# The beginning of the latents by tiles: first four tiles loaded, normalised and turned one by one

## What is computed

```
x = x + attn(layernorm(x))
    q_lat  = layernorm(x) @ Wq_down      # 512 -> 256
    kv_lat = layernorm(x) @ Wkv_down     # 512 -> 128
    k_pe   = layernorm(x) @ Wk_rope
    ...
x = x + ffn(layernorm(x))
```

## Time and profile before

| | |
|---|---|
| median of 3 runs | 1896.14 us (1895.67 to 1896.91) |
| the profiled execution's own time | 1895.38 us |
| its span in the profile | 1893.6 us |
| PE busy | 1834.3 us, 97% |
| DVE busy | 1337.8 us, 71% |
| ACT busy | 1036.3 us, 55% |
| POOL busy | 521.9 us, 28% |
| mean granted clock of TensorE | 0.992 |

### The profile page before, as it was taken

How to read it: one execution, slowest core, us unless ns; L and a number is a source line. 1 busy time by engine, 2 the same in 40 slices (tenths; PEclk the granted TensorE clock), 3 DMA queues, 4 the chain that set the end, 5 groups by cost and what they waited for, 6 DMA issues and landing times. The chain is left out here.

```text
span 1893.6 us, 30946 instructions
## 1 busy us (share of the span) xinstructions
PE 1834.3 (97%) x10898; PEld 1602.4 (85%) x10898; DVE 1337.8 (71%) x2818; ACT 1036.3 (55%) x2485; POOL 521.9 (28%) x314
## 2 busy tenths in 40 slices
PE   6899988999999999999999999999999799999998
PEld 4788876899999999999999999999999677777777
DVE  5466657888888888888888888888888633333333
ACT  2223326786777766676666666676666332223232
POOL 4466652120120154253244235234323000000000
PEclk9999999999999999999999999999999899999999
DMA  3399996422232121221221221212111150000000
GB/s 120 113 226 226 224 234 176 129 73 77 65 94 62 50 80 62 62 62 62 68 62 62 58 65 52 73 40 68 40 57 39 58 210 1 22 0 22 15 7 22
DMA packets 96625, 153.31 MB, mean 81 GB/s; under 512 B 12528, under 2 KB 46448, under 8 KB 96240
## 3 DMA queue, kind: packets, MB, share of 16 engines
q1 hardware_dynamic: 84976, 130.66, 23.5%
q10 hardware_dynamic: 11520, 20.98, 4.2%
HBM read 97.06 MB, written 54.53 MB: 80 GB/s over the span
## 5 line engine op out<-in xcount | busy, mean ns | idle before, releaser
L1140 ACT CAST turned_hi<-ps_turn 128x512 fp32r<-128x512 f32 (+1 forms) x576 | 312.8, 570 | 257.2 <-PE ps_turn L1325 253.3
L1096 ACT ACTIVATE probs<-ps_scores,bias 128x512 f32<-128x512 f32 (+3 forms) x640 | 401.0, 639 | 71.1 <-DVE bias L1184 70.9
L1223 DVE TENSOR_TENSOR turned_lo<-ps_turn,turned_hi 128x512 fp32r<-128x512 f32 (+1 forms) x576 | 375.0, 656 | 60.7 <-ACT turned_hi L1140 55.4
L1325 PE MATMUL ps_turn<-ident,probs 128*128 128x128 f32 x2176 | 300.9, 272 | 1.4 <-DVE turned_lo L1223 1.1
L1181 DVE TENSOR_REDUCE negmax<-ps_scores 128x1 f32<-128x512 f32 (+1 forms) x384 | 257.4, 675 | 44.9 <-PE ps_scores L1284 39.6
L1325 PEld LDWEIGHTS ps_turn<-ident,probs 128*128 128x128 f32 x2176 | 255.4, 140 | 33.5 <-issue 2.2
L1026 POOL TENSOR_TENSOR q_lo<-q_raw,q_hi 128x512 fp32r<-128x512 f32 x64 | 82.8, 1294 | 677.0 <-ACT q_hi L1088 677.0
L1284 PE MATMUL ps_scores<-k_hi,q_hi 128*128 128x512 f32 (+2 forms) x576 | 231.0, 401 | 4.5 <-ACT probs L1096 4.4
L1344 PE MATMUL ps_o<-turned_hi,kv_hi 128*128 128x256 f32 x1088 | 226.7, 285 | 0.0
L1344 PE MATMUL ps_o<-turned_lo,kv_hi 128*128 128x256 f32 x1088 | 223.6, 282 | 0.0
L1344 PE MATMUL ps_o<-turned_hi,kv_lo 128*128 128x256 f32 x1088 | 223.4, 282 | 0.0
(11 more groups left out here) (152 smaller groups left out, 3502.8 us busy)
## 6 DMA issues: line engine op xcount, KB each, us to landing
plainT<-plain_out ACTq DMA_DIRECT2D x64, 256.0 KB, 4.0
rotT<-rot_out SPq DMA_DIRECT2D x64, 256.0 KB, 4.3
all_signs<-signs SPq DMA_DIRECT2D x24, 512.0 KB, 2.8
q_raw<-plainT SPq DMA_DIRECT2D x128, 64.0 KB, 2.4
q_raw<-rotT SPq DMA_DIRECT2D x256, 32.0 KB, 2.1
signs<-in_W_up SPq DMA_DIRECT2D x16, 512.0 KB, 3.6
signs<-in_W_gate SPq DMA_DIRECT2D x16, 512.0 KB, 3.7
signs<-in_W_down SPq DMA_DIRECT2D x16, 512.0 KB, 3.6
```

Source lines behind the costliest of these rows:

```text
L1096: nc.scalar.activation(probs_of(n, i)[:, h, first_key:first_key + keys], ps_scores[:, pieces.number[args] % RING, 0:keys], ACT.Exp, scale= ...
L1140: nc.scalar.copy(turned[0][:, at, cols(*args)], ps_turn[:, bank, cols(*args)]).then_inc(turned_hi_ready, 1)
L1223: nc.vector.tensor_tensor(turned[1][:, at, cols(*args)], ps_turn[:, bank, cols(*args)], turned[0][:, at, cols(*args)].bitcast(F32), ALU.su ...
L1325: last = nc.tensor.transpose(ps_turn[:, bank, (2 * b + h) * P:(2 * b + h + 1) * P], probs_of(n, i)[:, h, key:key + P], ident[:])
```

## The change

- Chunk 0 of x is loaded by four DMAs of one tile each, with a semaphore each. SP's order is now tile 0, tile 1, the identity, the two latent weights, tile 2, tile 3, then chunks 1 to 3 as before and the pair weights.
- DVE handles chunk 0 tile by tile: statistics, aggregate, add, then after ACT's root the reciprocal and the normalisation, all on one column. Low parts of turned tiles stand between them, in an order written out by hand.
- ACT takes the four roots singly and splits the latent weights in two halves (768 columns each), put between roots and high parts. POOL subtracts by the same halves; PE waits for both.
- Chunk 1 is normalised on DVE, after its statistics, where POOL did it before. POOL normalises chunks 2 and 3.

The matmuls, their number and their order on PE are the same.

```diff
--- before.py
+++ after.py
@@ -99,6 +99,7 @@
         ps = ctx.enter_context(nc.psum_tensor("ps_lat", [P, 8, CH], F32))
 
         ident_loaded = sem("ident_loaded")
+        first_loaded = [sem(f"first_x_loaded{t}") for t in range(TC)]
         x_loaded = [sem(f"x_loaded{i}") for i in range(NC)]
         wlat_loaded = sem("wlat_loaded")
         pair_loaded = sem("pair_loaded")
@@ -135,16 +136,22 @@
 
         @block.sync
         def _(sp):
-            for c in range(NC):
+            def load_first(t):
+                sp.dma_start(x[:, t, :], hbm["x"].rearrange("(t p) d -> t p d", p=P)[t]).then_inc(first_loaded[t], 16)
+
+            load_first(0)
+            load_first(1)
+            sp.dma_start(ident[:], hbm["ident"]).then_inc(ident_loaded, 16)
+            sp.dma_start(w_raw[:, :, 0:QR],
+                         hbm["Wq_down"].rearrange("(k p) n -> p k n", p=P)).then_inc(wlat_loaded, 16)
+            sp.dma_start(w_raw[:, :, QR:QR + KVR],
+                         hbm["Wkv_down"].rearrange("(k p) n -> p k n", p=P)).then_inc(wlat_loaded, 16)
+            load_first(2)
+            load_first(3)
+            for c in range(1, NC):
                 rows = slice(TC * c, TC * (c + 1))
                 sp.dma_start(x[:, rows, :], hbm["x"].rearrange("(t p) d -> p t d", p=P)[:, rows, :]
                              ).then_inc(x_loaded[c], 16)
-                if c == 0:
-                    sp.dma_start(w_raw[:, :, 0:QR],
-                                 hbm["Wq_down"].rearrange("(k p) n -> p k n", p=P)).then_inc(wlat_loaded, 16)
-                    sp.dma_start(w_raw[:, :, QR:QR + KVR],
-                                 hbm["Wkv_down"].rearrange("(k p) n -> p k n", p=P)).then_inc(wlat_loaded, 16)
-                    sp.dma_start(ident[:], hbm["ident"]).then_inc(ident_loaded, 16)
             load_pair_weights(sp, hbm, pair_w, 0, pair_loaded)
 
         @block.vector
@@ -164,19 +171,49 @@
                 rows = slice(TC * c, TC * (c + 1))
                 nc.vector.tensor_scalar(std[:, rows], mv[:, rows, 1], LN_EPS, None, ALU.add).then_inc(var_ready, 1)
 
-                dve.wait_ge(std_ready, c + 1)
-                nc.vector.reciprocal(rstd[:, rows], std[:, rows]).then_inc(rstd_ready if c else rstd_done, 1)
-
-            for c in range(AHEAD):
-                for t in range(TC * c, TC * (c + 1)):
-                    tile_stats(t)
-                chunk_stats(c)
-                if c == 0:
-
-                    dve.wait_ge(rstd_done, 1)
-                    for t in range(TC):
-                        nc.vector.tensor_scalar(x[:, t, :], x[:, t, :], mv[:, t, 0:1], rstd[:, t:t + 1],
-                                                ALU.subtract, ALU.mult).then_inc(xn_ready, 1)
+                dve.wait_ge(std_ready, TC + c)
+                nc.vector.reciprocal(rstd[:, rows], std[:, rows]).then_inc(rstd_ready, 1)
+
+            def first_stats(t):
+                dve.wait_ge(first_loaded[t], 16)
+                nc.vector.bn_stats(bn[:, t, :], x[:, t, :]).then_inc(stats_done, 1)
+
+                dve.wait_ge(stats_done, 2 * t + 1)
+                nc.vector.bn_aggr(mv[:, t, :], bn[:, t, :]).then_inc(stats_done, 1)
+                dve.wait_ge(stats_done, 2 * t + 2)
+                nc.vector.tensor_scalar(std[:, t:t + 1], mv[:, t:t + 1, 1], LN_EPS, None, ALU.add).then_inc(var_ready, 1)
+
+            def first_norm(t):
+                dve.wait_ge(std_ready, t + 1)
+                nc.vector.reciprocal(rstd[:, t:t + 1], std[:, t:t + 1]).then_inc(rstd_done, 1)
+
+                dve.wait_ge(rstd_done, t + 1)
+                normalise(t)
+
+            def normalise(t):
+                nc.vector.tensor_scalar(x[:, t, :], x[:, t, :], mv[:, t, 0:1], rstd[:, t:t + 1],
+                                        ALU.subtract, ALU.mult).then_inc(xn_ready, 1)
+
+            def turned_low(t):
+
+                dve.wait_ge(xt_hi_ready, t + 1)
+                nc.vector.tensor_tensor(xT[1][:, :, t * P:(t + 1) * P],
+                                        ps[:, t % 2, :].rearrange("p (k n) -> p k n", k=KD),
+                                        xT[0][:, :, t * P:(t + 1) * P].bitcast(F32),
+                                        ALU.subtract).then_inc(xt_lo_ready, 1)
+
+            first_stats(0)
+            first_stats(1)
+            first_norm(0)
+            first_norm(1)
+            first_stats(2)
+            turned_low(0)
+            first_norm(2)
+            first_stats(3)
+            turned_low(1)
+            first_norm(3)
+            turned_low(2)
+            turned_low(3)
             for c in range(NC + 2):
                 for i in range(TC):
                     if c + AHEAD < NC:
@@ -187,16 +224,15 @@
                         nc.vector.scalar_tensor_tensor(lat(1, i, c - 1), ps[:, LAT0 + i, :], lat_scale(i),
                                                        lat(0, i, c - 1).bitcast(F32), ALU.mult,
                                                        ALU.subtract).then_inc(lat_lo_ready, 1)
-                    if c < NC:
-
-                        t = TC * c + i
-                        dve.wait_ge(xt_hi_ready, t + 1)
-                        nc.vector.tensor_tensor(xT[1][:, :, t * P:(t + 1) * P],
-                                                ps[:, t % 2, :].rearrange("p (k n) -> p k n", k=KD),
-                                                xT[0][:, :, t * P:(t + 1) * P].bitcast(F32),
-                                                ALU.subtract).then_inc(xt_lo_ready, 1)
+                    if 1 <= c < NC:
+                        turned_low(TC * c + i)
                 if c + AHEAD < NC:
                     chunk_stats(c + AHEAD)
+                if c == 0:
+
+                    dve.wait_ge(rstd_ready, 1)
+                    for t in range(TC, 2 * TC):
+                        normalise(t)
                 if c >= 2:
 
                     dve.wait_ge(kv_lo_turned, c - 1)
@@ -207,9 +243,11 @@
         @block.gpsimd
         def _(pool):
 
-            pool.wait_ge(wlat_hi_ready, 1)
-            nc.gpsimd.tensor_tensor(w[1][:], w_raw[:], w[0][:].bitcast(F32), ALU.subtract).then_inc(wlat_lo_ready, 1)
-            for c in range(1, NC):
+            for n, half in enumerate((slice(0, KD // 2), slice(KD // 2, KD))):
+                pool.wait_ge(wlat_hi_ready, n + 1)
+                nc.gpsimd.tensor_tensor(w[1][:, half], w_raw[:, half], w[0][:, half].bitcast(F32), ALU.subtract
+                                        ).then_inc(wlat_lo_ready, 1)
+            for c in range(2, NC):
 
                 pool.wait_ge(rstd_ready, c)
                 for t in range(TC * c, TC * (c + 1)):
@@ -224,27 +262,40 @@
         def _(act):
             def root(c):
                 rows = slice(TC * c, TC * (c + 1))
-                act.wait_ge(var_ready, c + 1)
+                act.wait_ge(var_ready, TC + c)
                 nc.scalar.activation(std[:, rows], std[:, rows], ACT.Sqrt).then_inc(std_ready, 1)
 
-            for c in range(AHEAD):
-                root(c)
-                if c == 0:
-
-                    act.wait_ge(wlat_loaded, 32)
-                    nc.scalar.copy(w[0][:], w_raw[:]).then_inc(wlat_hi_ready, 1)
+            def first_root(t):
+                act.wait_ge(var_ready, t + 1)
+                nc.scalar.activation(std[:, t:t + 1], std[:, t:t + 1], ACT.Sqrt).then_inc(std_ready, 1)
+
+            def turned_high(t):
+                act.wait_ge(xt_ready, t + 1)
+                nc.scalar.copy(xT[0][:, :, t * P:(t + 1) * P],
+                               ps[:, t % 2, :].rearrange("p (k n) -> p k n", k=KD)).then_inc(xt_hi_ready, 1)
+
+            def split_lat(half):
+                nc.scalar.copy(w[0][:, half], w_raw[:, half]).then_inc(wlat_hi_ready, 1)
+
+            first_root(0)
+            first_root(1)
+            turned_high(0)
+            first_root(2)
+            act.wait_ge(wlat_loaded, 32)
+            split_lat(slice(0, KD // 2))
+            turned_high(1)
+            first_root(3)
+            split_lat(slice(KD // 2, KD))
+            turned_high(2)
+            turned_high(3)
             for c in range(NC + 2):
                 for i in range(TC):
                     if 1 <= c <= NC and i < NL:
                         act.wait_ge(lat_ready, NL * (c - 1) + i + 1)
                         nc.scalar.activation(lat(0, i, c - 1), ps[:, LAT0 + i, :], ACT.Copy,
                                              scale=lat_scale(i)).then_inc(lat_hi_ready, 1)
-                    if c < NC:
-
-                        t = TC * c + i
-                        act.wait_ge(xt_ready, t + 1)
-                        nc.scalar.copy(xT[0][:, :, t * P:(t + 1) * P],
-                                       ps[:, t % 2, :].rearrange("p (k n) -> p k n", k=KD)).then_inc(xt_hi_ready, 1)
+                    if 1 <= c < NC:
+                        turned_high(TC * c + i)
                 if c + AHEAD < NC:
                     root(c + AHEAD)
                 if c >= 2:
```

(2 more changed lines are left out.)

## The result

The changed kernel takes **1892.36 us** (median of 20 runs, 1887.54 to 1895.40), the kernel before, in 20 runs beside it, 1895.81 us (1891.01 to 1899.62). The ratio is 0.998, with an interval of 0.9973 to 0.9987: 3.45 us less, between 2.5 and 5.1. The profiled execution took 1893.47 us with a span of 1891.7, so 1.9 us less than that of before, 1895.38.

What follows compares the result with a forecast made beforehand. PE, busy 97% of the span, bounds the kernel, so only its idle time at the beginning can go. The first latent matmul moving 3.6 us earlier, against the median 1896.14, gave 1892.5 us, range 1891.0 to 1894.4.

Steps and rivals of the forecast that it cites:

- What bounds the start: Beginning of the kernel: DVE stands about 3.1 us behind POOL's subtraction of the latent weights, delaying the first latent matmul.
- Tiles 0 and 1: First loads: landing near 4.4 and 5.1 us, normalised by 7.9; placed late by 0.3 us, nothing changes.
- Tile 2: Load of x tile 2: lands at 8.33 us, its statistics running 8.37 to 9.05.
- Rival (d): Tile 2 lands at 9.0 us or later, DMAs costing over 0.1 us each; gain 2.9, 1893.2 us; chance 0.05.
- The add of tile 3: DVE's one-element epsilon add at 11.68 us, inside POOL's first half: held, ending at 12.30; free it costs 0.17.
- rival (a): Tile 3's one-element add is not held: PE begins at 15.85, gain 4.1, 1892.1 us; chance 0.27.
- The normalisations: DVE's normalisations of tiles 2 and 3 start 0.18 us before POOL's halves and take 0.54 us each.
- Rival (b): A normalisation loses the race against POOL and is held: 1.7 us lost, gain 1.9, 1894.2 us; chance 0.11.
- The start: First latent matmul on PE at 16.30 us instead of 19.91, 3.6 us earlier.
- The cover of the fifth tile: Tile 4, normalised by DVE at about 19.7 to 20.3 us, is wanted by PE at 21.1: cover 0.8 us.
- rival (c): Low-clock stretches shift: one fewer gives 5.2 (1890.9 us), chance 0.06; one more gives 2.0 (1894.1), chance 0.07.
- Rival (e): PE falls to 1.2 GHz in holes between chunks, 1.6 us each; slower from three further stretches; chance 0.02.

Runs made afterwards that it cites:

- the best version: Changed kernel with all four tiles before the weights, tiles 2 and 3 turned into idle banks, weights split into query and key-value columns: 1888.68 us, ratio 0.9957 to kernel before.

## Why the prediction came out as it did

The time, 1892.36, was forecast as 1892.5, and the gain, 3.45 us, as 3.6. That the start carries the gain was right; that the numbers agree to 0.15 us is luck beside an interval of 2.5 to 5.1. Step by step:

- **What bounds the start** held. One wait on POOL returns about 3.0 us, where the prediction read about 3.1 from the earlier trace rows.
- **Tiles 0 and 1** landed at 3.48 and 4.13, not 4.4 and 5.1. The back-reckoning from 6.43 at 381 GB/s took the transfer of 1 MB for four small ones in a row. As the prediction said of an error here, nothing followed: DVE was free at 6.9 and waited 1.50 us for tile 2. But that the early loads buy only finished work was too little: with the loads of before, DVE came 0.26 us later against POOL and lost the race.
- **Tile 2** landed at 8.40, forecast 8.33. But this profiled execution was the luckiest of six with this order of loads: the others had 8.55, 8.92, 9.00, 9.07 and 9.55, while x in the old order landed between 6.10 and 6.40 in all of three. Every tenth goes straight into the start, 7.17 us later. Rival (d), tile 2 at 9.0 or later, was given 0.05; by size it happened in three of the six, and nearly in a fourth. The mean of the six is 8.92, which takes 0.5 us off the gain of the profiled execution. What spreads the landing stays open. The term was right in one trace and its spread was missing from the working.
- **The add of tile 3** was the step that failed. Forecast held to 12.30 (0.6 us), it took 0.15 from 11.63: rival (a). The row it rested on had three elements, and the two-column run shows that the number of elements was the difference. Small size alone does not save an instruction: two elements were held.
- **The normalisations** won their race, with a lead of 0.33 us where 0.18 was forecast: they came 0.07 sooner and POOL 0.08 later. Rival (b) was real all the same: 0.26 us fewer, in the run with the old loads, and it was lost.
- **The start**: forecast 16.30, rival (a) 15.85, measured 15.60. Of the 0.25 us beyond (a), 0.10 is that the low part starts 0.07 after the start of the add and not 0.17, and 0.09 that the turn starts 0.60 after the start of the normalisation and not 0.69; the rest is hundredths. In the second execution it was 16.20.
- **The cover of the fifth tile**: forecast 0.8 us. Normalised by 19.45 and turned at 20.16: 0.7. With POOL in DVE's place the cover is gone, and 1.0 us was lost in one of two executions.
- **The hole of 2.33 us** stayed, forecast near 30.8, found at 29.96.
- **The clock, behind the hole**: the stretch there, assumed to move along, was at full clock in this execution, and low again in others (0.80 and 0.63 us a matmul at 27.68 in the best version). So the first half of rival (c) came: the gain rose from 4.5 us ahead of that stretch to 5.8 behind it, 1.3 returned where 1.6 was reckoned. It did not last. Of this, 1.2 us were lost again between 75 and 86 us, where both traces have a low stretch of 3.4 us (from 75.4 in before, 77.3 in after).
- **The clock, near 1500 us**: the low stretch there was longer by 6.8 us and took 2.3 us. An earlier arrival doesn't by itself lengthen that stretch: it was 13.7 us in before and in the run with the whole split, which reach the 9000th matmul within 0.4 us of each other, but also in the best version with the chunk on POOL, 6.1 us ahead; and one kernel, the change with its second chunk on POOL, had 20.5 and 23.9 us in its two executions. What sets it stays open.
- **The clock, at the start**: the level is read from the matmuls' durations alone: the windows 15 to 20 and 20 to 30 us of before show a granted clock of 1.00, though matmuls of 0.63 us stand in them, as long as those in the stretch that shows 0.51.
- **The medians** don't follow the start closely: with the start 3.2 us earlier 5.1 came out (2.7 to 6.6), with 3.7 to 4.3 earlier 3.45 (2.5 to 5.1), and with 6.7 earlier 6.9 (5.5 to 10.6). None needs a loss to explain it, and none shows that there is no loss.
- **Rival (e)** did not come: the holes between chunks keep their lengths, and the kernel is faster.

So the sum was near for two reasons that cancel in part: the work behind the add began 0.6 us sooner than forecast (11.70 for 12.32), and tile 2 lands about 0.5 us later on the mean of six executions than in the profiled one. The second was not foreseen.

## What to carry to other kernels

When a short VectorE instruction has one very long sibling, look at what GpSimd ran beside it, and first try the cheapest cure, a wait or an order that lets VectorE pass first: here one line gave about 3.0 us of the 3.7 to 4.3 that a rewrite of the whole beginning gave at the start, and no less in time. After each such cure read the releaser of the first dependent matmul again: it moved from x to the weights, and from there on a landing 0.3 us sooner was enough to move it back. Where a gain at the start is less than the scatter of the runs, judge it by the timeline of several executions, and put the spread of a landing into the sum, not its one value.

## What the runs showed of the hardware

- **A VectorE instruction that is held waits for the whole of GpSimd's.** Held were a normalisation (2.42 and 2.16 us for 0.55, and 3.65 in the kernel before), which ended 0.27 to 0.29 us after GpSimd's instruction, and the two-element add (0.84), which ended 0.03 after it. Beside the same GpSimd work the reciprocal (0.15), the statistics (0.69), the aggregate (0.18), the one-element add (0.15) and the subtraction that reads PSUM (0.68) kept their times.
- **Being first in the record by 0.07 us is not enough.** A normalisation with that lead was held; with 0.27 (the third of the kernel before, at 10.79, POOL at 11.06) and with 0.33 none was. The GpSimd instruction that came second was hardly longer: a half of the weights took 1.88 to 1.89 us there, and 1.80 to 1.81 where no normalisation was ahead of it. The Trainium skill, "SBUF — State Buffer", SBUF: two separate sides, says that whichever starts first has the shared ports for its whole instruction; the runs agree down to some tenths of a microsecond, but a recorded start need not be the moment at which the ports are taken.
- **The landings behind a queue of small transfers scatter.** With five DMAs of 64 to 512 KB issued ahead of it, tile 2 landed anywhere from 8.40 to 9.55 us in six executions of one order, and the 1 MB of x, issued first and as one DMA, between 6.10 and 6.40 in three. With the identity third, the four tiles, in the version with the weights split by use, landed at 3.40, 4.03, 6.32 and 6.96 us, the identity's 64 KB at 5.08. With the identity first it landed at 2.63, and the query weights at 8.63 instead of 9.28 and 9.54. The identity was first in one execution only, so that a small transfer among the first causes the scatter is a hint and not shown.
- **When PE comes to full speed after its start varies, and it changes what an experiment shows.** From the first latent matmul to the first of 0.40 us or less it was 4.3 us before, 3.9 and 3.8 in the changed kernel's two executions, 3.1 with all tiles ahead of the weights, and about 6.2 in the runs with the whole split and with the old loads. With the second chunk on DVE, that chunk came 14.0 us after the start where the rise took 3.1 us, 14.3 to 14.6 where it took 3.8 to 4.3, and 15.1 to 15.4 where it took about 6. With the chunk on POOL it came after 15.3 to 15.4 us in all three executions, whether the rise took 3.1 us or 6.3. So, compared across these versions, moving it to DVE is worth up to 1.4 us where PE comes up early, and nothing where it comes up late.
